# Query and key weights multiplied first: reordering the projection stage in front of a long cross-attention

## What is computed

```python
x = x + _L0_xattn_ref(_layernorm(x), ctx, ctx, fside, fside, fside, Wq, bq, Wk, bk, Wv, bv, ...)

Q = q_in @ Wq.T + bq          # q_in: 512 x 512, normalised tokens
K = k_in @ Wk.T + bk          # k_in: 8192 x 512, the context
V = v_in @ Wv.T + bv
att = jnp.einsum('bsd,btd->bst', Q, K) * scale
att = att + beta_risk * phi_risk + beta_prio * phi_prio - beta_impl * phi_impl
w = jax.nn.softmax(att, axis=-1)
```

## Time and profile before

| | us |
|---|---|
| median of 3 runs | 705.48 |
| lowest, highest | 705.48, 706.05 |
| span of the profiled execution, first to last instruction | 703.8 |
| median less that span | 1.7 |
| TensorE busy | 693.6 |
| VectorE busy | 557.0 |
| ScalarE busy | 337.1 |
| GpSimd busy | 196.8 |

### The profile page before, as it was taken

How to read it: one execution, slowest core, us unless ns; L and a number is a source line. 1 busy time by engine, 2 the same in 40 slices (tenths; PEclk the granted TensorE clock), 3 DMA queues, 4 the chain that set the end, 5 groups by cost and what they waited for, 6 DMA issues and landing times.

```text
span 703.8 us, 9942 instructions
## 1 busy us (share of the span) xinstructions
PE 693.6 (99%) x3237; PEld 574.2 (82%) x3237; DVE 557.0 (79%) x702; ACT 337.1 (48%) x451; POOL 196.8 (28%) x144
## 2 busy tenths in 40 slices
PE   7999999999999999999999999999999999999997
PEld 7888888888888788888888888888888788788885
DVE  6778887877989998899996653769434799899897
ACT  4322222222245565566663333742233588887872
POOL 4335444454440000000000000426785111211245
PEclk9999999999999999999999999999999999999999
DMA  8046667767642236433210701614200899999984
GB/s 310 7 151 207 227 216 244 231 223 242 230 162 90 89 120 248 169 105 104 89 60 1 283 1 63 240 48 163 99 2 2 306 342 344 394 394 360 407 301 150
DMA packets 38686, 130.70 MB, mean 186 GB/s; under 512 B 6658, under 2 KB 10756, under 8 KB 35588
## 3 DMA queue, kind: packets, MB, share of 16 engines
q1 hardware_dynamic: 35828, 124.45, 49.0%
q0 software_dynamic: 1536, 4.20, 1.8%
q10 hardware_dynamic: 1296, 1.71, 0.7%
HBM read 120.89 MB, written 9.46 MB: 185 GB/s over the span
## 4 chain that ended last, share of the span: by engine, by line
PE 91%; DMA 2%; DVE 2%; POOL 2%; issue 1%; ACT 1%; POOLq 0%; DVEq 0%; ACTq 0%
PE ps L927 25%; PE ps L894 8%; PE ps L890 8%; PE ps L891 8%; PE ps L826 5%; PE ps L828 5%; PE ps L827 5%; PE ps L1140 4%; PE ps L1110 4%; PE ps L1121 3%; PE ps L1119 3%; PE ps L1120 3%; POOL met L488 1%; PE ps L1045 1%; DMA slots<-y_out 1%
## 5 line engine op out<-in xcount | busy, mean ns | idle before, releaser
L431 POOL TENSOR_TENSOR c_lo<-ring,c_hi 128x512 fp32r<-128x512 f32 x64 | 85.6, 1338 | 102.3 <-ACT c_hi L548 102.3
L548 ACT ACTIVATE c_hi<-ring 128x512 fp32r<-128x512 f32 x64 | 40.4, 633 | 128.1 <-PE ps L894 102.8
L890 PE MATMUL ps<-qk_hi,c_hi 128*128 128x512 f32 x256 | 100.2, 392 | 0.1
L891 PE MATMUL ps<-qk_lo,c_hi 128*128 128x512 f32 x256 | 99.6, 389 | 0.0
L436 POOL TENSOR_TENSOR w_lo<-raw,w_hi 128x1024 fp32r<-128x1024 f32 x11 | 26.7, 2431 | 260.5 <-ACT w_hi L675 246.5
L1305 DVE TENSOR_TENSOR runmax<-runmax,att 128x512 f32<-128x512 f32 x64 | 91.2, 1426 | 6.0 <-DVE att L1299 3.2
L1614 DVE TENSOR_TENSOR wu_lo<-raw_u,wu_hi 128x2048 fp32r<-128x2048 f32 (+1 forms) x33 | 69.7, 2112 | 15.3 <-ACT wu_hi L685 15.0
L894 PE MATMUL ps<-qk_hi,c_lo 128*128 128x512 f32 x256 | 68.4, 389 | 0.0
L1299 DVE SCALAR_TENSOR_TENSOR att<-ring,beta,ps 128x512 f32 (+1 forms) x64 | 47.8, 747 | 23.5 <-PE ps L894 22.9
L927 PE MATMUL ps<-p_hi,d_hi 128*128 128x512 f32 x256 | 64.2, 393 | 0.1
L927 PE MATMUL ps<-p_hi,d_lo 128*128 128x512 f32 x256 | 63.3, 389 | 0.0
(11 more groups left out here) (305 smaller groups left out, 1478.4 us busy)
## 6 DMA issues: line engine op xcount, KB each, us to landing
ring<-stream SPq DMA_DIRECT2D x64, 512.0 KB, 3.6
raw_u<-up_in SPq DMA_DIRECT2D x22, 1024.0 KB, 7.2
raw_d<-down_in SPq DMA_DIRECT2D x33, 512.0 KB, 7.3
ring<-ctx_in SPq DMA_DIRECT2D x32, 512.0 KB, 3.3
raw<-shared_in SPq DMA_DIRECT2D x11, 768.0 KB, 5.5
raw_u<-up_last_in SPq DMA_DIRECT2D x11, 768.0 KB, 6.8
slots<-blank SPq DMA_DIRECT2D x15, 256.0 KB
late<-wqkv_in SPq DMA_DIRECT2D x1, 3072.0 KB, 10.2
```

The source lines that it names most:

```text
L431: pool.tensor_tensor(c_lo[:, s % 2, :], ring1[:, s, 0, :], c_hi[:, s % 2, :].bitcast(F32), ALU.subtract).then_inc(lo1_ready, 1)
L548: act.activation(c_hi[:, s % 2, :], ring1[:, s, 0, :], ACT.Copy).then_inc(hi1_ready, 1)
L890: pe.matmul(ps[:, s, :], hi, qk_hi[:, k, :], start=(k == 0), stop=False)
L891: pe.matmul(ps[:, s, :], hi, qk_lo[:, k, :], start=False, stop=False)
```

## The change

The product of the two weights, M = Wq^T Wk times the scale, is made first (48 products on PSUM banks 0 to 3), and the transposed normalised tokens are multiplied with it (48 products on banks 4 to 7). The loads are reordered: chunk k of both weights share a semaphore, chunks 0 and 1 are issued ahead of the tokens. The query bias becomes a column per chunk (bq_wk, multiplied with ones on TensorE, L928 of the changed kernel, then qk_bias, added in qk_hi and qk_lo). The key bias becomes a row bk_wq, spread over the partitions by a product with ones after the second context tile (L937, L938), and reduced against the normalised tokens on VectorE in context tiles 4 to 7 (key_bias). wk_hi and wk_lo move to VectorE (L1322, L1326), the application of the norm to ScalarE (L551), x += bv to GpSimd (L448). One of the three runs of filler products is left.

```diff
-WARM = (6, 3, 4)
+WARM = 6
...
         @block.sync
         def _(sp):
-            for st in range(0, ST, 2):
+            def load_x(st):
                 sp.dma_start(x[:, st, :], x_in[st * P:(st + 1) * P, :]).then_inc(x_loaded[st], 16)
-            for k in range(0, KC, 2):
-                sp.dma_start(wq[:, k, :], wq_in[:, k, :]).then_inc(wq_loaded[k], 16)
-            for k in range(0, KC, 2):
-                sp.dma_start(wk[:, k:k + 2, :], wk_in[:, k:k + 2, :]).then_inc(key_loaded, 16)
+            def load_wq(k):
+                sp.dma_start(wq[:, k, :], wq_in[:, k, :]).then_inc(weights_loaded[k], 16)
+            def load_wk(k):
+                sp.dma_start(wk[:, k, :], wk_in[:, k, :]).then_inc(weights_loaded[k], 16)
+            load_wq(0)
+            load_wq(1)
+            load_x(0)
+            load_wq(2)
+            load_wk(2)
+            load_x(2)
+            load_x(3)
+            load_wq(3)
+            load_wk(3)
+            sp.dma_start(cols[:, 0:16], cols_in).then_inc(key_loaded, 16)
+            sp.dma_start(betas[:, :], betas_in.to_broadcast([P, 3])).then_inc(key_loaded, 16)
...
             step(pool.affine_select(out=ident[:, :], in_=ident[:, :], compare_op=ALU.not_equal, fill=1.0,
                                     base=0, pattern=[[-1, P]], channel_multiplier=1))
             step(pool.memset(ones[:, :], 1.0))
+            pool.sem_inc(consts_ready, 1)
...
-            pool.wait_ge(ln_ready, ST)
             for k in range(KC):
                 pool.wait_ge(wqhi_ready, k + 1)
                 pool.tensor_tensor(wq_lo[:, k, :], wq[:, k, :], wq_hi[:, k, :].bitcast(F32),
                                    ALU.subtract).then_inc(wqlo_ready, 1)
-            for k in range(0, KC, 2):
-                pool.wait_ge(wkhi_ready, k // 2 + 1)
-                pool.tensor_tensor(wk_lo[:, k:k + 2, :], wk[:, k:k + 2, :], wk_hi[:, k:k + 2, :].bitcast(F32),
-                                   ALU.subtract).then_inc(wklo_ready, 1)
+            pool.wait_ge(late_small, 32)
+            pool.wait_ge(ln_ready, ST)
+            for st in range(ST):
+                pool.tensor_tensor(x[:, st, :], x[:, st, :], bv_b[:, :], ALU.add).then_inc(bv_added, 1)
...
         @block.scalar
         def _(act):
-            for st in range(1, ST, 2):
-                act.dma_start(x[:, st, :], x_in[st * P:(st + 1) * P, :]).then_inc(x_loaded[st], 16)
-            for k in range(1, KC, 2):
-                act.dma_start(wq[:, k, :], wq_in[:, k, :]).then_inc(wq_loaded[k], 16)
-            act.dma_start(cols[:, 0:16], cols_in).then_inc(key_loaded, 16)
-            act.dma_start(betas[:, :], betas_in.to_broadcast([P, 3])).then_inc(key_loaded, 16)
+            for k in range(2):
+                act.dma_start(wk[:, k, :], wk_in[:, k, :]).then_inc(weights_loaded[k], 16)
+            act.dma_start(x[:, 1, :], x_in[P:2 * P, :]).then_inc(x_loaded[1], 16)
...
+            act.wait_ge(consts_ready, 1)
+            act.activation(any_root[:, :], ident[:, 0:1], ACT.Sqrt)
+            wq_high(0)
+            wq_high(1)
             root(1, 0, 0)
+            wq_high(2)
             root(1, 1, 1)
...
+            normal(1, 0, 0)
+            normal(1, 1, 1)
             evacuate_lnT(1, 0, 0, lna_hi, 4)
             root(1, 2, 2)
...
             evacuate_lnT(1, 1, 1, lna_hi, 4)
+            wq_high(3)
             root(1, 3, 3)
...
+            normal(1, 2, 2)
+            normal(1, 3, 3)
             evacuate_lnT(1, 2, 2, lna_hi, 4)
...
             evacuate_lnT(1, 3, 3, lna_hi, 4)
...
+            for d in range(KC):
+                act.wait_ge(m_psum, d + 1)
+                act.activation(m_hi[:, d, :], ps[:, d, :], ACT.Copy, scale=SCALE).then_inc(mhi_ready, 1)
             def ctx_high(g, s):
                 act.wait_ge(s_psum, g * U + (s + 1))
                 act.wait_ge(ring1_full[s], g * 16 + 16)
                 act.activation(c_hi[:, s % 2, :], ring1[:, s, 0, :], ACT.Copy).then_inc(hi1_ready, 1)
...
             ctx_high(0, 0)
             ctx_high(0, 1)
+            act.wait_ge(bias_terms, 2)
             for d in range(KC):
                 act.wait_ge(qk_psum, d + 1)
...
                     pe.matmul(ps[:, bank, 0:P], ones[:, :], ident[:, :], start=True, stop=True)
             pe.wait_ge(consts_ready, 1)
...
+            keep_warm(WARM, 7)
+            def weight_term(k, d, a, b, opening=False, ended=False):
+                return pe.matmul(ps[:, d, :], a[:, k, d * P:(d + 1) * P], b[:, k, :], start=opening, stop=ended,
+                                 skip_group_check=True)
+            def weight_high(k):
+                pe.wait_ge(wqhi_ready, k + 1)
+                pe.wait_ge(wkhi_ready, k + 1)
+                for d in range(KC):
+                    weight_term(k, d, wq_hi, wk_hi, opening=(k == 0))
+            def weight_low_key(k):
+                pe.wait_ge(wklo_ready, k + 1)
+                for d in range(KC):
+                    weight_term(k, d, wq_hi, wk_lo)
+            def weight_low_query(k):
+                pe.wait_ge(wqlo_ready, k + 1)
+                for d in range(KC):
+                    weight_term(k, d, wq_lo, wk_hi)
             for k in range(2):
...
+                weight_high(k)
+                weight_low_key(k)
+                weight_low_query(k)
+            pe.wait_ge(consts_ready, 2)
+            weight_high(2)
+            turn_ln(1, 0, 0, ln_a, 4)
+            weight_low_key(2)
+            turn_ln(1, 1, 1, ln_a, 4)
+            weight_low_query(2)
+            def weight_ended(d):
+                weight_term(KC - 1, d, wq_hi, wk_hi)
+                weight_term(KC - 1, d, wq_hi, wk_lo)
+                weight_term(KC - 1, d, wq_lo, wk_hi, ended=True).then_inc(m_psum, 1)
+            pe.wait_ge(wqhi_ready, KC)
+            pe.wait_ge(wkhi_ready, KC)
+            pe.wait_ge(wklo_ready, KC)
+            pe.wait_ge(wqlo_ready, KC)
+            weight_ended(0)
+            weight_ended(1)
+            turn_ln(1, 2, 2, ln_a, 4)
+            weight_ended(2)
+            turn_ln(1, 3, 3, ln_a, 4)
+            weight_ended(3)
+            def query_term(k, d, a, b, opening=False, ended=False):
+                return pe.matmul(ps[:, 4 + d, :], a[:, k, d * P:(d + 1) * P], b[:, k, :], start=opening, stop=ended,
+                                 skip_group_check=True)
             pe.wait_ge(lnT_ready, ST)
...
             pe.wait_ge(lnT_lo_ready, ST)
...
+            for k in range(KC - 1):
+                pe.wait_ge(mhi_ready, k + 1)
+                for d in range(KC):
+                    query_term(k, d, m_hi, lna_hi, opening=(k == 0))
+                for d in range(KC):
+                    query_term(k, d, m_hi, lna_lo)
+                pe.wait_ge(mlo_ready, k + 1)
+                for d in range(KC):
+                    query_term(k, d, m_lo, lna_hi)
+            pe.wait_ge(bias_terms, 1)
+            pe.wait_ge(mlo_ready, KC)
             for d in range(KC):
...
+                mm = pe.matmul(ps[:, 0, d:d + 1], bq_wk[:, d * P:(d + 1) * P], ones[:, 0:1], start=True, stop=True)
+            mm.then_inc(bias_psum, 1)
+            for d in range(KC):
+                query_term(KC - 1, d, m_hi, lna_hi)
+                query_term(KC - 1, d, m_hi, lna_lo)
+                query_term(KC - 1, d, m_lo, lna_hi, ended=True).then_inc(qk_psum, 1)
+            def spread_bias():
+                pe.wait_ge(bias_terms, 3)
+                pe.matmul(ps[:, 6, 0:1], ones[:, :], bias_dot[:, :], start=True, stop=True)
+                pe.matmul(ps[:, 7, :], ones[:, :], bk_wq[:, :], start=True, stop=True).then_inc(bias_psum, 1)
...
-            with pe.Fori(0, EARLY // U) as g:
+            pe.wait_ge(bias_terms, 2)
+            for s in range(U):
+                scores(0, s, first=(s == 0))
+                if s == 1:
+                    spread_bias()
+            with pe.Fori(1, EARLY // U) as g:
                 for s in range(U):
-                    scores(g, s, first=(s == 0))
+                    scores(g, s)
             for t in range(EARLY, CT):
                 scores(t // U, t % U)
                 if t == EARLY:
-                    for q in range(ST):
-                        pe.matmul(ps[:, 6, q:q + 1], qb[:, q * P:(q + 1) * P], ones[:, 0:1], start=True, stop=True)
...
+            def key_high(k):
+                dve.wait_ge(weights_loaded[k], 32)
+                dve.tensor_copy(wk_hi[:, k, :], wk[:, k, :]).then_inc(wkhi_ready, 1)
+            def key_low(k):
+                dve.wait_ge(wkhi_ready, k + 1)
+                dve.tensor_tensor(wk_lo[:, k, :], wk[:, k, :], wk_hi[:, k, :].bitcast(F32), ALU.subtract).then_inc(wklo_ready, 1)
+            def first_moments(st):
                 dve.wait_ge(x_loaded[st], 16)
                 moments(st)
...
+            for k in range(2):
+                key_high(k)
+                key_low(k)
+            first_moments(0)
+            first_moments(1)
+            scales(1, 0, 0)
+            key_high(2)
```

(49 more changed lines are left out.)

125 lines of the change are left out of this document (30 added, 95 removed).

## The result

| us | before | after |
|---|---|---|
| median of 6 runs each, on one chip | 705.48 | 707.52 |
| lowest, highest | 704.74, 706.05 | 706.75, 708.00 |
| span of the profiled execution | 703.8 | 705.8 |

After over before is 1.0032, 95% interval 1.0022 to 1.0041: slower by 2.3 us (1.6 to 2.9), 2.0 us between the two spans. The forecast was 706.8 in a range of 704.4 to 708.8, with 0.42 on "slower by over 0.2%".

A forecast was written before the change was run, and what follows sets the result against it. TensorE, busy 99% of 703.8 us, was taken as the bound. Terms +1.3, +1.06, -0.8 gave +1.6, cut to +1.3 for a possible first turn: span 705.1, median 706.8 us, range 704.4 to 708.8.

The forecast's parts named there:

- First chunks: Program start: weight pairs land at 4.2 and 5.5, products begin at 5.0, TensorE waits 0.6 us before the third chunk.
- the half of 0.5 us: At 5.5 us VectorE may win the first turn against GpSimd, saving up to 0.5; half was taken off the sum.
- Fourth chunk: Weight product: ScalarE's late copy, then GpSimd's subtraction until 18.6; TensorE, through at 16.7, waits 1.9 us.
- Token products: Products of the weight product with the transposed tokens: begin at 23.1, TensorE through at 34.8.
- The bias row: VectorE makes bk_wq, 2.9 us, ahead of qk_lo: second context tile starts at 39.7 against 38.44, +1.3 us.
- Behind the mark: Work after the second context tile's start: spread +1.06, old column products -0.8, reductions, bv_b additions and loads hidden.
- Spread: Two fp32 products spreading the biases after the second context tile, 0.2 and 0.86 us: +1.06.
- The four column products: The old kernel's four column products on TensorE near 169 us leave: -0.8 us.
- their rival: VectorE's new reductions stall the context loop in tiles 4 to 7: +2 us, 708.8, chance 0.09.
- The sum: +1.3, +1.06 and -0.8 make +1.6; with half the possible turn gain taken, +1.3 us on the profiled span, 705.1.
- The clock rival: Early weight products run at TensorE's lower clock: +0.9 us (707.7), at worst +2.5 (709.3); chance 0.16.
- Never waiting: TensorE never waits once begun: token products at 18.9 instead of 23.1, 4.2 us less, 702.6; chance 0.17.

The follow-up runs named there:

- both edits: Changed kernel with bk_wq made behind the four qk_lo and ScalarE's fourth query chunk copy moved ahead of its transposed-tile copies; 704.70 us, ratio 0.9992 to the old kernel.
- early high part without key bias: Changed kernel with the fourth query chunk's high part made early and no bk_wq, spread or reductions; 703.74 us, ratio 0.9982 to the old kernel.
- early high part: Changed kernel with only ScalarE's copy of the fourth query chunk moved ahead of its copies of the transposed tiles; 706.02 us, ratio 1.0014 to the old kernel.

## Why the prediction was nearly right, and where it was off

**First chunks.** The turns of VectorE and GpSimd were as worked out from the earlier trace rows: wk_lo of the second chunk lasts 1.69 beside GpSimd's 1.29. The first two pairs were put at 4.2 and 5.5 and had landed at 5.27 and 7.03, so products began at 5.95 and not 5.0. The third chunk's cast still ended at 13.05 where 13.0 was predicted, and that is partly luck: VectorE won the first turn (wk_lo 0.69 from 5.73, while GpSimd's first subtraction, from 5.98, took 1.59), where the working had it lose, and this made up for most of the late landings. Beyond that, the half of 0.5 us that was credited for the turn was not had.

The wait ahead of the third chunk was put at 0.6 and was 1.44, though the cast came on time: the 24 products ahead of it were counted at the lower speed until about 10, so to end by 12.4, and ran at the higher one all through, to 11.8. In the seven of nine profiles in which they began slowly, TensorE did not wait there at all.

Missed was which operation GpSimd holds up. The working had the cast wait; it was one of 128 numbers in front of it, nmr, that took 1.01 instead of the 0.16 it takes alone, and the cast stands behind it. The Trainium skill (SBUF — State Buffer, section "SBUF: two separate sides") makes no exception for size: the blocked side waits out the whole instruction. These rows agree, and I had applied it to the large operations alone. The trace of the kernel before shows it too, for an addition of 128 numbers beside GpSimd's subtractions of 2.4 us each:

```profile
16.83 4.76 POOL L425 TENSOR_TENSOR wk_lo<-wk,wk_hi 128x1024 fp32r<-128x1024 f32 x2
...
17.14 2.13 DVE L1270 TENSOR_TENSOR beta<-betas 128x1 f32<-128x1 f32 x1
```

**Fourth chunk.** Its start was predicted at 18.6 with a wait of 1.9 by ScalarE's order; it was measured at 18.80 and 1.72, and undoing the order gave 1.3 us (ratio 0.0018). Token products were predicted at 23.1 and came at 23.46. TensorE was to be through at 34.8; the last issue is at 35.16, which by the spacing of 0.227 makes 35.4.

**The bias row.** Predicted +1.3 at the second tile, measured +1.49 there: the row, whose last three operations start at 33.42, ends at 35.75 (35.5) and the rest follows. Moving it alone gave 0.0017. The chain was right. Its price was not: 1.8 us by the prediction (39.7 less 37.9), 1.3 by the experiment, since TensorE's own end (35.4, not 34.8) is next behind it.

**Behind the mark.** Spread 1.06, measured 1.11. The four column products: -0.8, measured -0.59 between these two profiles and -0.82 between the two of the old kernel. The reductions against the tokens were put at 1.0, between 0.69 and 1.75; one takes 0.69 and a read of 0.08, and no TensorE idles beside them (the windows above), so their rival fell. The first of the four and its read, timeline of VectorE:

```profile
54.77 0.69 DVE L1387 CUSTOM_DVE_ANT_0 bk_ln<-ln_a,ps 128x512 f32<-128x512 f32 x1
55.39 0.08 DVE L1387 DVE_READ_ACCUMULATOR2_ANT nbias<- 128x1 f32 x1
```

**The sum.** +1.3 was predicted, +1.99 came. The step that was mis-sized is the sum at the mark and behind it: +1.50 for +1.3, -0.59 for -0.8, and the 0.3 taken off for the first turn (together 0.7). It carried the result across the bound of 0.2% that the forecast had stood just inside of; "slower" had 0.42, "same" 0.43, and the measured 0.32% is of the first.

**The clock rival.** It was priced at +0.9 to +2.5, for 17 or more slow products, with the wait ahead of the third chunk already taken off (13.9 and 15.2 against 13.0). The slow start does happen: of the nine profiles of the changed kernel and its versions with six fillers or none, seven have the first eight products at the lower level (2.04 to 2.08 us and 1.91 for four) and two, that of the changed kernel itself among them, have not. What was wrong is how long it lasts: in none of them beyond the twelfth product. Where eight or nine were slow, TensorE came to the third chunk 0.32 to 0.34 us after VectorE's cast instead of 0.15 (no filler, both edits, no key bias); where more were, 0.66 (early high part without key bias) and 0.97 (early high part). But for the filler, all five have the changed kernel's orders up to there, so an execution of the changed kernel can lose up to 0.8 us at this place, but no profile of it shows that.

In the old kernel there is no such cover, and its two profiles, with the loads within 0.14 us of each other, start the run of twenty 0.8 us apart. So the old kernel pays in full for a late clock and the changed one for a part; the spans say +2.0 against the later start of the old one, and +2.8 (705.8 less 703.0) against the other; the ratio of many runs, 2.3, lies between.

**Never waiting** had 0.17 and asked for token products before 20.4. The earliest of any version here is 21.30.

## What to carry to other kernels

Work that is moved to the front starts earlier only as far as its slowest preparation: 5.6 us of earlier start went mostly into waits, one because the splits of two weight matrices met on the same two engines, one because a copy stood late in ScalarE's order. Bring every VectorE operation with two SBUF inputs, however small, and the casts too, into the turns with GpSimd, and look at what is queued behind it. A cost with a wait behind it is nearly free until that wait is mended: price it again after each edit. And a side term such as a bias row belongs where the engine has slack, not ahead of what the next stage waits for.
